# Three decays before the second direction's exponentials on ScalarE, three scans before all its sums on VectorE, and 36 dummy transposes for 50

## What is computed

```python
def _mamba_dir(xz, conv_w, conv_b, xproj_w, dtproj_w, dt_bias, A_log, Dp):
    ...
    delta = jax.nn.softplus(delta + dt_bias[None, :, None])
    A = -jnp.exp(A_log)
    dA = jnp.exp(jnp.einsum('bdl,dn->bdln', delta, A))
    dBx = jnp.einsum('bdl,bnl,bdl->bdln', delta, Bm, u)
    h = _ssm_scan(dA, dBx)
    y = jnp.einsum('bdln,bnl->bdl', h, Cm)
    y = y + Dp[None, :, None] * u
    return y * jax.nn.silu(z)
...
out_f = _mamba_dir(xz, ...)
out_b = _mamba_dir(xz[:, :, ::-1], ...)[:, :, ::-1]
```

## Time and profile before

| | |
|---|---|
| time, median of 3 runs | 346.17 us (345.65 to 346.56) |
| the profiled execution's own time | 345.95 us |
| its span, first to last instruction | 343.6 us |
| mean granted clock of TensorE | 0.976 of full speed |
| busy share of the span | PE 90%, DVE 85%, ACT 73%, POOL 58%, PEld 57% |
| scans (VectorE) | 128, 146.0 us in all |
| products `dBx` (GpSimd) | 64, 150.6 us in all |

### The profile page before, as it was taken

The page is one execution under the profiler, slowest core; times in us unless marked ns, Lnnn a source line. Parts: engine busy times, 40 slices in busy tenths (PEclk is TensorE's granted clock), DMA queues, the critical chain, the costliest instruction groups (busy, mean ns, idle before and its releaser), DMA issues.

```text
span 343.6 us, 5759 instructions
## 1 busy us (share of the span) xinstructions
PE 308.1 (90%) x1818; PEld 194.8 (57%) x1818; DVE 291.5 (85%) x498; ACT 250.6 (73%) x465; POOL 197.8 (58%) x132
## 2 busy tenths in 40 slices
PE   6999957999999999899999999998889998699980
PEld 5544556555665564444554454584356566499970
DVE  2778799999999999999999999766968989781483
ACT  2669996999899998999999999627567767312331
POOL 7600656999999998898898987302000001460154
PEclk9999989999999999999999999999999999969996
DMA  6996111322313133133232200000000000015010
GB/s 156 327 289 226 45 62 63 115 92 101 116 69 124 61 123 122 63 123 103 83 122 87 99 0 1 2 0 1 2 0 2 2 2 1 18 47 140 9 34 22
DMA packets 15377, 26.23 MB, mean 76 GB/s; under 512 B 1971, under 2 KB 8908, under 8 KB 15348
## 3 DMA queue, kind: packets, MB, share of 16 engines
q1 hardware_dynamic: 14580, 24.76, 22.8%
q0 software_dynamic: 768, 1.11, 1.1%
HBM read 23.49 MB, written 2.51 MB: 76 GB/s over the span
## 4 chain that ended last, share of the span: by engine, by line
PE 45%; DVE 32%; issue 8%; POOL 7%; ACT 5%; DMA 1%; SPq 0%; POOLq 0%; DVEq 0%; ACTq 0%
PE bank L730 23%; DVE arena L1249 23%; POOL arena L451 5%; PE bank L774 4%; PE bank L959 3%; DVE acc L1259 3%; PE bank L872 3%; PE bank L796 2%; PE bank L1117 2%; PE bank L1109 2%; PE bank L978 2%; PE bank L762 2%; ACT arena L680 2%; DMA cw<-in_L_attn_convb_w 1%; ACT arena L661 1%
## 5 line engine op out<-in xcount | busy, mean ns | idle before, releaser
L451 POOL TENSOR_TENSOR arena<-arena,k_maskT 128x1024 f32<-128x1024 f32 x64 | 150.6, 2390 | 36.5 <-DVE arena L1236 19.7
L1249 DVE TENSOR_TENSOR_SCAN arena<-bank,arena 128x512 f32<-128x512 f32 x128 | 146.0, 1199 | 0.0
L730 PEld LDWEIGHTS bank<-ident,arena 128*128 128x128 f32 x718 | 77.6, 141 | 82.3 <-DVE arena L1249 55.8
L730 PE MATMUL bank<-ident,arena 128*128 128x128 f32 x718 | 104.0, 281 | 15.1 <-DVE arena L1249 9.4
L557 ACT ACTIVATE bank<-delta,a_neg 128x508 f32<-128x508 f32 x128 | 88.3, 692 | 6.7 <-DVE arena L1249 5.9
L872 PE MATMUL bank<-conv_in_T,ident 128*128 128x512 f32 x192 | 92.8, 593 | 0.0
L601 ACT ACTIVATE conv_in_T<-bank,c_col 128x256 f32<-128x256 f32 x192 | 80.3, 472 | 11.4 <-PE bank L730 10.6
L872 PEld LDWEIGHTS bank<-conv_in_T,ident 128*128 128x128 f32 x192 | 31.6, 191 | 15.8 <-issue 15.0
L463 POOL TENSOR_SCALAR rstd<-moments 128x4 f32<-128x4 f32 x4 | 0.9, 234 | 63.0 <-DVE moments L1301 63.0
L1259 DVE SCALAR_TENSOR_TENSOR acc<-bank,c_col,acc 128x256 f32<-128x256 f32 x64 | 27.3, 467 | 0.6 <-PE bank L730 0.4
L730 PE MATMUL bank<-ident 128*128 128x128 f32 x145 | 22.5, 332 | 5.4 <-DVE acc L1156 3.8
(11 more groups left out here) (174 smaller groups left out, 325.6 us busy)
## 6 DMA issues: line engine op xcount, KB each, us to landing
k_maskT<-b_rows SPq DMA_DIRECT2D x32, 512.0 KB, 3.7
w_sb<-in_L_ffn_w SPq DMA_DIRECT2D x1, 2048.0 KB, 9.4
dispatched_tokens<-zeros SPq DMA_DIRECT2D x1, 650.0 KB, 17.7
x_tok<-in_x SPq DMA_DIRECT2D x1, 512.0 KB, 4.2
ctx_tok<-in_ctx SPq DMA_DIRECT2D x1, 512.0 KB, 4.4
out<-uT SPq DMA_DIRECT2D x1, 512.0 KB, 4.3
arena<-dispatched_tokens SPq DMA_DIRECT2D x2, 130.0 KB, 2.3
arena<-dispatched_tokens SPq DMA_DIRECT2D x1, 260.0 KB, 3.4
```

The lines of the kernel that those rows point to most:

```text
L451: gp.tensor_tensor(dBx[g % 2][h], du[:, dr, h, :], b_bc[:, g % RING, :], ALU.mult).then_inc(dBx_ok, 1)
L730: return pe.transpose(dst, src, ident[0:src.shape[0], 0:src.shape[0]])
L1249: ve.tensor_tensor_scan(o, a, v, 0.0, ALU.mult, ALU.add).then_inc(scanned, 1)
```

## The change

ScalarE makes the decays 0 to 2 ahead of the two `exp_abs(1, h)` and the decays 3 to 5 behind them; the loop's first step makes none. VectorE runs the scans 0 to 2 ahead of both `add_rest(1, h)` and of the copy of `skip`, which now stand together ahead of `sum_y(0, 0)`. GpSimd waits in step 1 for all four banks of the second direction, where it waited for two in step 1 and two in step 2. TensorE runs 20 dummy transposes once the second of these banks has been read (`d101`, the end of the first `add_rest`) and 16 behind the first eight real transposes, both into bank 6, where it ran 50 into bank 3 once `skip` was copied.

```diff
             if n == scan_from:
-                held_at_scan, holder = holder[0:Y_BANK], [None] * Y_BANK + holder[Y_BANK:]
+                held_at_scan, holder = list(holder), [None] * Y_BANK + holder[Y_BANK:]
...
             def dbx_step(g, dr):
 
                 gp.wait_ge(b_in[g % RING], 16 * (g // RING + 1))
-                if g in (1, 2):
-                    for th in range(2):
-                        wait_read(gp, f"d1{g - 1}{th}")
+                if g == 1:
+                    for h in range(NH):
+                        for th in range(2):
+                            wait_read(gp, f"d1{h}{th}")
...
             sc.preload_act_table(ACT.Exp)
+            sc.wait_ge(a_ok, 1)
+            for k in range(DA_BANKS):
+                decay(k)
             for h in range(NH):
                 exp_abs(1, h)
-            sc.wait_ge(a_ok, 1)
-            for k in range(DA_BANKS):
+            for k in range(DA_BANKS, 2 * DA_BANKS):
                 decay(k)
...
-                decay(4 * g + 3)
+                if g:
+                    decay(4 * g + 3)
...
-                if g < STEPS - 1:
+                if 0 < g < STEPS - 1:
                     decay(4 * g + 4)
...
-                if g < STEPS - 1:
+                if 0 < g < STEPS - 1:
                     decay(4 * g + 5)
...
-            wait_read(pe, held_at_scan[HT_BANK])
-            keep_busy(HT_BANK, 50)
+            wait_read(pe, "d101")
+            keep_busy(where["d101"][0], 20)
             for g in range(STEPS):
                 pe.wait_ge(scanned, 4 * g + 2)
                 for b in (0, 2):
                     turn_pair(g, b)
+                if g == 0:
+                    keep_busy(where["d101"][0], 16)
...
-            add_rest(1, 0)
-            evacuate("skip", acc[:, :, :], lambda ap: tiles(ap, VB))
             for dr in range(2):
                 wait_read(ve, f"c{dr}")
             for g in range(STEPS):
                 for i in range(4):
                     if g == 0 and i == 3:
-                        add_rest(1, 1)
+                        for h in range(NH):
+                            add_rest(1, h)
+                        evacuate("skip", acc[:, :, :], lambda ap: tiles(ap, VB))
```

## The result

The changed kernel takes 347.37 us (median of 13 runs, 346.79 to 348.14) against 345.65 us (13 runs, 344.97 to 346.82) for the kernel before: 1.0044 times as long, with a 95% interval of 1.0030 to 1.0057. The profiled execution took 347.52 us, with a span of 345.4.

The account below looks back on a forecast made before the run. GpSimd's product for step 12 was taken to bind: 2.5 us late less 1.19 to spare gives + 1.3 on 345.95, 347.25; with 0.22 for the median 347.47, said as 347.4 us, range 346.4 to 348.4.

Parts of the forecast that it names:

- What bounds it: First direction's scan loop: GpSimd hardly ahead of the scans, tightest at step 12's second product.
- 1.19 us to spare at step 12: Kernel before: step 12's second product ends at 115.01 us, scan 49 starts at 116.20; least of all steps.
- GpSimd's restart: GpSimd waits for both `add_rest`: step 1 starts at 52.5 us instead of 46.57, step 2 2.5 us later.
- a term that was too small: Loop start: edges cleared from 41.57 us, first scan starts at about 42.4.
- The sum: Scan 49: 2.5 us late less 1.19 to spare, 1.3 us later; chance of GpSimd late by 2.5 us, 0.68.
- VectorE's own path: Up to scan 3: 54.4 us, 1.2 us earlier taken alone; as rival setting the end, 344.75 us, chance 0.11.
- the dearer end that was given (4.0): TensorE's 20 dummies: 2 us all at full clock level to 4 all at the low one.
- the first one: VectorE's wait for GpSimd at step 1: product ready at 57.2 us, scan 5 due near 56.7.
- The clock did stay low: Rival, TensorE's clock low into the loop: + 1.6 to + 3.8 us, in the middle 348.65 us, chance 0.06.
- a sign of being wrong: Profile after: step 12 ready by 116 us, VectorE without such idle time, or TensorE at 0.50 in the loop.
- The price that it gave for a whole low step: TensorE in the loop: one whole step at the low clock level costs 2.8 to 5.0 us.
- The lock: VectorE and GpSimd lock each other out for a whole instruction: 0.91 us seen once, up to 2.3 us each time.

Follow-up runs that it names:

- the wait alone: Kernel before with one edit, GpSimd waits for all four second-direction banks in step 1: 347.68 us against 345.8, 1.0064.
- the extras later: Changed kernel with GpSimd's four extra second-direction instructions ahead of steps 6, 10, 14, 16 instead of 3, 6, 9, 12: 345.32 us against 345.8, 0.9991.
- without dummies: Changed kernel without its 36 dummy transposes: 346.87 us against 345.8, 1.0031.
- the version that beats both: Changed kernel, GpSimd's wait at step 2 only, `skip` copied before `add_rest`, four transposes ahead of 20 dummies, no others: 344.06 us against 345.44, 0.9955.
- no wait: Changed kernel with GpSimd's wait for the second direction's banks removed: 347.87 us against 345.44, 1.0065.
- the old waits: Changed kernel with GpSimd's waits put back, two banks in step 1 and two in step 2: 346.9 us against 345.8, 1.0022.
- the last one of the experiments: The version that beats both, with the four extra instructions ahead of steps 6, 10, 14, 16: 343.99 us against 345.44, 0.9957.

## Why the prediction was right, point by point

*What bounds it.* Right. The 1.19 us to spare at step 12 was the number on which all hung; the wait alone costs what step 2 comes late less that, and moving the extras takes it away.

*GpSimd's restart.* 52.5 us was expected, 53.12 came. Of the 0.62 us, 0.46 lie ahead of the change: the edges were cleared at 42.03 us in this execution instead of 41.57, and with the extras later, where they were cleared at 41.51, GpSimd went on at 52.60. The rest is a term that was too small: the first scan starts 1.03 us behind the MEMSETs, not 0.83. From there all went as worked out: 65.0 us from the restart to the end of step 12's product (53.12 to 118.14, and 52.5 to 117.5 in the prediction), with no stall between.

*The sum.* + 1.3 us was expected and + 1.72 measured on the medians, + 1.5 (1.0 to 2.0) by the ratio. What the sum lacked is this 0.16 to 0.2 us and the 0.09 us from a product's end to its scan, which it had at nothing. The two make + 1.6. That the forecast of 347.4 us met the 347.37 so closely is luck: it stood on a median of 346.17 us for the kernel before, which is 345.65 over 13 runs, so a base 0.52 us too high made up for a difference 0.42 us too small. The difference is what the working can be judged by.

*VectorE's own path.* This step failed, though it did not reach the end. Scan 3 was to start at 54.4 us, 1.2 us earlier than before. It started at 55.95; less the 0.46 us that this execution began late that is 55.5, 0.1 us earlier than before. The scans and both `add_rest` came as said (0.68 us instead of 1.60 for the first instruction), and the copy of `skip` ended at 53.46, but the sums then waited 1.69 us for TensorE. TensorE's timeline and stretches answer to the earlier trace rows:

```profile
49.74 4.53 PE L734 MATMUL bank<-ident 128*128 128x128 f32 x20 [4.45 <-DVE early_weights L1227]
54.06 1.72 PE L734 MATMUL bank<-ident,arena 128*128 128x128 f32 x8
55.61 1.91 PE L734 MATMUL bank<-ident 128*128 128x128 f32 x16
```

```profile
49.80:52.80 3.00, 3.00 (x15) 0.50 0.00 0
53.00:56.00 3.00, 3.00 (x18) 0.59 0.00 0
56.00:59.00 3.00, 3.00 (x24) 1.00 0.05 12
```

All 20 dummies ran at the low level and took 4.53 us, half a microsecond beyond the dearer end that was given (4.0), and the first real transposes were slow too. The waits for GpSimd in the loop are therefore 1.55 us and not 2.5: the rest of the lead went to TensorE before it could go to GpSimd. None was needed at step 1, where the prediction had the first one. In the kernel with the extras later the same 20 dummies took 4.39 us and scan 3 came at 54.88.

*The rivals.* VectorE's own path did not set the end. The clock did stay low to between 55 and 56 us, a little into the loop, and without dummies to past 62, and the end did not move: it was covered, as the prediction said, by the wait for GpSimd, though without dummies with 0.19 us left. So TensorE at 0.50 in the loop, which the prediction named as a sign of being wrong, was seen at the loop's start and was no such sign. The price that it gave for a whole low step, 2.8 to 5.0 us, was too high for VectorE's path: without dummies the low level lasted from the first transposes to the end of step 1, more than one whole step, and VectorE waited 2.9 us for TensorE in all, at the sums of the steps 0, 1 and 3 (of the 1.27 us at step 0 some 0.8 would be there at the full level too, by the 0.64 us from the first transposes, here at 53.28, to the sums).

*The lock.* The prediction took the 0.91 us of the earlier trace rows as the price of a lock and the rest of a product, up to 2.3 us, as its bound by the Trainium skill (SBUF — State Buffer, Who interferes with whom). The measured prices are 0.31 and 0.44 us (the version that beats both, with the extras later and without), 1.04 and 2.02 (no wait) and 2.04 (the old waits), within the bound. The row was the wrong guide to the size: it showed the tail of one product. Where products stand in a row, the second instruction of `add_rest` pays nearly a whole one, whether the first has paid (1.04 us with no wait) or not (the old waits). So in the changed order the new wait buys 2.0 us of VectorE's time against the old waits and 3.1 against none, where the row of the kernel before shows 0.91. The forecast did not hang on this, since it compares with the kernel before, where the price was that 0.91.

*Seen in the trace as announced:* one idle piece of GpSimd, waits at the steps 3, 6, 9 and 12, 0.68 instead of 1.60 us, a product that ends just ahead of scan 49. Not as announced: no wait at step 1, waits of 1.55 us in all instead of 2.5, the trace names "issue" as the releaser, and scan 49 came at 118.23 us instead of 117.5.

## What to carry to other kernels

An engine at 57% of the span can set the end of a stage: measure for each product how long it lies ready before its reader starts, and compare the smallest of these distances with what an edit takes from its engine. A wait that keeps one engine from slowing another is paid by everything queued behind it, so put it at the instruction that would collide and no earlier: the version that beats both does so, among its edits, and pays 0.44 us for the product that it lets run. Before taking work off an engine that is late, look whether some of it can stand behind the point where it is late.

## What the runs showed of the hardware that was not expected

GpSimd and VectorE seem to take turns where both have several instructions in a row. In the kernel without a wait, with GpSimd's products back to back, the TENSOR_SCALAR of 0.67 us lasted until 0.55 us behind the running product (45.89 to 47.60, the product to 47.05), and the TENSOR_TENSOR of 1.23 us, which follows in 0.03 us, lasted until 1.1 us behind the next one (to 50.88, the product to 49.81). These are the two products:

```profile
44.68 2.37 POOL L448 TENSOR_TENSOR arena<-arena,k_maskT 128x1024 f32<-128x1024 f32 x1
47.00 2.81 POOL L448 TENSOR_TENSOR arena<-arena,k_maskT 128x1024 f32<-128x1024 f32 x1
```

So the next product went ahead of the TENSOR_TENSOR, as a turn each would have it; that reading is argued from these ends. First come, first served fits them as well, since the row of that product starts at 47.00 us and that of the TENSOR_TENSOR at 47.63. The products are lengthened in turn: the second one here took 2.81 us for 2.35, and three of them took 8.20 us in the kernel with the old waits, where three take 7.0 in the version that beats both.

```profile
49.68 8.20 POOL L451 TENSOR_TENSOR arena<-arena,k_maskT 128x1024 f32<-128x1024 f32 x3 [7.11 <-DVE early_weights L1226]
```

The same dummies behind the same wait do not take the same time: 50 took 7.34, 7.35 and 8.32 us in the three kernels that ran them, and 20 took 3.73 to 4.53 us in the six kernels that ran them (3.73 in the last one of the experiments). The Trainium skill (TensorE: Matmul & The Clock Gate, the part on the HAM clock gate) says that the moment at which the clock rises varies from run to run, and these rows agree: where the 50 took 8.32 us the granted clock was 0.50 until past 52 us, in the earlier trace rows until 50.4. Where dummies stand ahead of the path, as in the kernel before, this is 1 us of its time that comes and goes (first sums at 54.81 and 55.72 us, spans of 343.6 and 344.6).
